# A spectral block kernel on one core: the height transform back in three runs of 128 channels instead of four of 96, and the second biases moved to a map added to x

## The reference, cut to what matters

```python
v    = group_norm(x, 32 groups)                 # mean and variance over pixels and 12 channels
bias = v @ bias_w.T + bias_b
xf   = rfftn(v.reshape(B, H, W, 4, 96), axes=(1, 2), norm='ortho')
r1 = relu(xr @ w1[0] - xi @ w1[1] + b1[0])      # per block of 96 channels
i1 = relu(xr @ w1[1] + xi @ w1[0] + b1[1])
r2 = r1 @ w2[0] - i1 @ w2[1] + b2[0]
i2 = r2 @ w2[1] + i1 @ w2[0] + b2[1]            # r2, not r1: the imaginary part uses the new real part
out = x + irfftn(complex(r2, i2), norm='ortho') + bias
```

## Time and profile before

| | us |
|---|---|
| three executions | 445.85, 444.65, 444.74 |
| median | 444.74 |
| span of the profiled execution, first to last instruction | 443.0 |
| median less that span | 1.7 |
| mean granted TensorE clock | 0.981 of full speed |
| PE busy | 411.8 (93%) |
| PE weight loads busy | 375.5 (85%) |
| DVE busy | 318.4 (72%) |
| ACT busy | 239.8 (54%) |
| POOL busy | 7.2 (2%) |
| DMA | 32.5 MB, mean 73 GB/s |

### The profile page before, as it was taken

How to read it: one execution, slowest core, us unless ns; L and a number is a source line. 1 busy time by engine, 2 the same in 40 slices (tenths; PEclk the granted TensorE clock), 3 DMA queues, 4 the chain that set the end, 5 groups by cost and what they waited for, 6 DMA issues and landing times.

```text
span 443.0 us, 17840 instructions
## 1 busy us (share of the span) xinstructions
PE 411.8 (93%) x7832; PEld 375.5 (85%) x7832; DVE 318.4 (72%) x772; ACT 239.8 (54%) x568; POOL 7.2 (2%) x13
## 2 busy tenths in 40 slices
PE   4468699989999999999999999999999999998996
PEld 4457699889998899888998899888998899987894
DVE  3679895759776876769767786768857687668734
ACT  2654785257742685438752586438752577425620
POOL 0131000000000000000000000000000000000000
PEclk9759899999999999999999999999999999999999
DMA  7570000170004300170003500161002600030004
GB/s 216 164 216 2 2 1 4 63 261 3 3 23 157 148 1 5 38 285 3 3 12 123 194 1 4 38 243 45 2 5 88 236 1 4 27 155 3 4 4 144
DMA packets 11645, 32.50 MB, mean 73 GB/s; under 512 B 4196, under 2 KB 5904, under 8 KB 11568
## 3 DMA queue, kind: packets, MB, share of 16 engines
q1 hardware_dynamic: 11568, 31.36, 20.1%
HBM read 15.63 MB, written 12.58 MB: 64 GB/s over the span
## 4 chain that ended last, share of the span: by engine, by line
PE 81%; issue 7%; DVE 6%; SPq 2%; POOL 2%; ACT 1%; DVEq 0%; POOLq 0%
PE bank L535 81%; SPq L490 1%; DVE r L1022 1%; DVE z L947 1%; DVE rsum L1015 1%; SPq L495 1%; POOL g L806 1%; ACT biasw L857 1%; DVE o_sb L1037 0%; DVE rho L947 0%; POOL g L807 0%; ACT z L863 0%; ACT yraw L823 0%; DVE extreme L1175 0%; DVE extreme L1180 0%
## 5 line engine op out<-in xcount | busy, mean ns | idle before, releaser
L535 PE MATMUL bank<-biasw,y 128*64 128x384 f16 x1152 | 108.8, 335 | 0.0
L535 PEld LDWEIGHTS bank<-biasw,y 128*64 128x64 f16 x1152 | 93.5, 196 | 1.7 <-DVE rsum L1015 0.3
L535 PEld LDWEIGHTS bank<-w2s,rho 96*64 96x64 f16 (+1 forms) x3072 | 81.4, 109 | 4.4 <-issue 2.5
L535 PE MATMUL bank<-w2s,rho 96*64 96x96 f16 (+1 forms) x3072 | 84.5, 207 | 0.0
L863 ACT ACTIVATE z<-bank 128x384 f16<-128x384 f32 x72 | 35.2, 488 | 60.5 <-PE bank L535 59.9
L535 PE MATMUL bank<-w1R,y 128*32 128x96 f16 (+3 forms) x768 | 60.1, 228 | 7.6 <-ACT y L843 3.2
L848 ACT ACTIVATE g<-bank 128x384 f16<-128x384 f32 x64 | 31.0, 484 | 64.2 <-PE bank L535 64.2
L535 PE MATMUL bank<-tab,x_sb 128*128 128x128 f32 x384 | 52.5, 291 | 11.2 <-DMA x_sb<-in_x 6.6
L535 PEld LDWEIGHTS bank<-tab,x_sb 128*128 128x128 f32 x384 | 48.3, 201 | 14.6 <-issue 7.4
L947 DVE SCALAR_TENSOR_TENSOR rho<-bank,rho 96x64 f16<-96x64 f32 (+1 forms) x128 | 50.6, 431 | 10.9 <-PE bank L535 9.2
L947 DVE SCALAR_TENSOR_TENSOR z<-bank,z 128x384 f16<-128x384 f32 x72 | 39.9, 557 | 25.6 <-ACT z L863 25.2
(11 more groups left out here) (102 smaller groups left out, 379.0 us busy)
## 6 DMA issues: line engine op xcount, KB each, us to landing
x_sb<-in_x SPq DMA_DIRECT2D x16, 768.0 KB, 7.1
out<-o_sb SPq DMA_DIRECT2D x14, 768.0 KB, 3.8
y<-y SPq DMA_DIRECT2D x24, 128.0 KB, 2.7
out<-o_sb SPq DMA_DIRECT2D x8, 192.0 KB, 1.9
tab<-in_tab SPq DMA_DIRECT2D x1, 642.0 KB, 5.9
o_sb<-in_bias_wt SPq DMA_DIRECT2D x4, 144.0 KB, 2.8
b1s<-in_b1h SPq DMA_DIRECT2D x1, 384.0 KB, 5.3
o_sb<-in_w SPq DMA_DIRECT2D x2, 144.0 KB
```

The source lines that it names most:

```text
L535: return nc.tensor.matmul(o, lhsT, rhs, start=start, stop=stop, **kw)
```

## The change

1. p4 takes `r` in three runs of 128 channels, not four of 96. There are 6 steps of 12 matmuls (72 an image) and two last steps. `rho` has 128 partitions; its tiles are three runs for each half of the units, so the middle tile holds channels of two blocks.
2. The last two steps (unit 8) become, for each half, two groups of 12 matmuls of 96 columns: first four pieces of 64 partitions (`WIDE_PIECES`), then four of 32 (`SMALL_PIECES`), 48 an image. The table `xi` is 192 wide, not 132.
3. The second weights follow: `w2s` is 128 rows in 4 slots, zero where a channel isn't of the block. `c2_rho` still has 48 matmuls of 96 columns for each gi (24 more for gi = 0), now 128 rows high. The w2 products are 16, not 8. DVE makes all forms, in 12 instructions; POOL's three are gone.
4. b2 and bias_b leave the weights and `rho`. At the start PE makes a map from them (5 matmuls, f32), DVE writes it to `added` (4 instructions), and POOL adds it to x in place, two instructions for each image, as soon as p1 of that image has read x. `add_x` waits for it. The marks' 8 loads are replaced by 3 loads, at the same place in SP's queue.
5. PE waits for those loads and for DVE's `shift_rows` before image 0. POOL's copy and memset before the second maximum, and DVE's two copies in `second_scales`, are gone. DVE's memsets at the start change tiles (zeros for the new forms, for `rhoX` and for the last 32 partitions of the two short units of `r`), and the table loaded at line 491 grows from 326 to 583 words a partition.

The core of the diff:

```diff
+WIDE_PIECES = ((0, 0, 64, 0, 0, 0), (1, 0, 64, 0, 1, 32), (1, 64, 128, 1, 0, 0), (2, 64, 128, 1, 1, 32))
+SMALL_PIECES = ((0, 64, 96, 0, 0, 64), (0, 96, 128, 0, 1, 0), (2, 0, 32, 1, 0, 64), (2, 32, 64, 1, 1, 0))
...
         def w2_loads():
+            for tile, first, last, k, ri, ch in LOAD_PIECES:
+                of = w2[ri].rearrange("(p k) c n -> k c p n", k=2)[k][ch:ch + last - first]
+                yield w2raw[first:last, :, tile, :], of
...
             load(1, 1)
-            for dst, src in mark_loads():
-                sp.dma_start(dst, src).then_inc(marks_in, 16)
+            with nc.allow_non_contiguous_dma(reason="one column of 96 per block"):
+                for dst, src in shift_loads():
+                    sp.dma_start(dst, src).then_inc(shift_in, 16)
...
             def p4(b, p, more, first):
-                for j in range(10):
-                    if j == 4:
+                for j in range(8):
+                    if j == 3:
                         c2_bias(b, p, 0 if more else 2, more, first)
...
-                    if j in (0, 4, 8):
-                        pe.wait_ge(rh_ready, 9 * b + min(j + 4, 9))
-                        pe.wait_ge(rl_ready, 9 * b + min(j + 4, 9))
+                    if j in (0, 3, 6):
+                        pe.wait_ge(rh_ready, 9 * b + (4, 8, 9)[j // 3])
+                        pe.wait_ge(rl_ready, 9 * b + (4, 8, 9)[j // 3])
...
+                            o = bank.rearrange("k (c u m) -> k c u m", u=4, m=4)[:, :, t, :]
+                            last = mm3(o, [r[:, s, u, 128 * ti:128 * ti + 128] for s in range(2)],
+                                       [heightT[:, s, int(u in SHORT_UNITS), :] for s in range(2)], True, True, skip_group_check=True)
                     else:
-                        for c in range(2):
-                            blk = 2 * (j - 8) + c
-                            last = mm3(bank[0:BC, 132 * c:132 * c + 132], [r[:, s, 8, BC * blk:BC * blk + BC] for s in range(2)],
-                                       [xi[:, s, :] for s in range(2)], True, True)
+                        half = j - 6
+                        for pieces in (WIDE_PIECES, SMALL_PIECES):
+                            for of, w in ((0, 0), (0, 1), (1, 0)):
+                                for tile, first_row, last_row, k, ri, ch in pieces:
...
             pe.wait_ge(w2_in, 16 * N_W2)
...
+            last.then_inc(w2_prod, 1)
+            pe.wait_ge(shift_in, 16 * N_SHIFT)
+            pe.wait_ge(added_ready, 1)
+            mm(c_bank[2][:, 0:CH], T("impulse", 2), b2rows[:, :], True, False, skip_group_check=True)
+            for blk in range(BLOCKS):
+                last = mm(c_bank[2][:, BC * blk:BC * blk + BC], b2row0[:, blk, :], w2imag[:, blk, :], False, blk == BLOCKS - 1, skip_group_check=True)
+            last.then_inc(shift_prod, 1)
             image(0, 0, first=True)
...
-            pool.wait_ge(w2_in, 16 * N_W2)
-            pool.wait_ge(consts_in, 16)
-            do(nc.gpsimd.tensor_copy(w2_form(0, BC, 0), by_group(w2raw[0:BC, :, 0, :])))
-            do(nc.gpsimd.tensor_scalar(w2_form(0, BC, 1), by_group(w2raw[0:BC, :, 1, :]), -1.0, None, ALU.mult))
-            do(nc.gpsimd.tensor_scalar(w2_form(BC, 3, 0), by_group(w2raw[BC:BC + 3, :, 0, :]), rowscale[BC:BC + 3, :], None, ALU.mult))
             pool.wait_ge(second_largest, 2)
-            do(nc.gpsimd.tensor_copy(extreme[BC:BC + 3, 4:5], extreme[BC:BC + 3, 2:3]))
-            do(nc.gpsimd.memset(extreme[BC:BC + 3, 2:3], 0.0))
             pool.wait_ge(s1_ready, 1)
-            do(nc.gpsimd.tensor_tensor(extreme[:, 2:5], extreme[:, 2:5], coef[:, 2:5], ALU.mult))
-            do(nc.gpsimd.tensor_scalar(extreme[:, 3:5], extreme[:, 3:5], s1[:, :], None, ALU.mult))
-            all_peak(extreme[:, 2:5], peaks2[:, :])
+            do(nc.gpsimd.tensor_tensor(extreme[:, 2:4], extreme[:, 2:4], coef[:, 2:4], ALU.mult))
+            do(nc.gpsimd.tensor_scalar(extreme[:, 3:4], extreme[:, 3:4], s1[:, :], None, ALU.mult))
+            all_peak(extreme[:, 2:4], peaks2[:, :])
+
+            pool.wait_ge(added_ready, 6)
+            for b in range(BATCHES):
+                pool.wait_ge(y_prod, Y_ITEMS * (b + 1))
+                tiles = x_sb[b % 2]
+                nc.gpsimd.tensor_tensor(tiles[:, 0, :], tiles[:, 0, :], added[:, 0, :], ALU.add).then_inc(x_shifted, 1)
+                nc.gpsimd.tensor_tensor(tiles[:, 1:TILES, :], tiles[:, 1:TILES, :], added[:, 1:2, :].to_broadcast([128, TILES - 1, CH]), ALU.add).then_inc(x_shifted, 1)
...
+            def shift_rows():
+                dve.wait_ge(shift_in, 16 * N_SHIFT)
+                row0 = T("row0", BC).rearrange("k (o m) -> k o m", o=1).to_broadcast([BC, BLOCKS, 128])
+                nc.vector.tensor_tensor(b2row0[:, :, :], row0, b2col[:, :].rearrange("k (b o) -> k b o", o=1).to_broadcast([BC, BLOCKS, 128]),
+                                        ALU.mult).then_inc(added_ready, 1)
...
             for ct in range(NT):
                 y_low(0, 0, ct)
             second_forms()
+            shift_rows()
+            shift_all()
             image(0, 0, first=True)
```

More of the change, by code:

```diff
@@ L188, in constants @@
     put("const", np.broadcast_to(const, (128, 64)))
[L189 to L206, removed]
+    sign = np.ones((128, 3))
+    for tile, first, last, _, ri, _ in LOAD_PIECES:
+        if ri:
+            sign[first:last, tile] = -1
+    put("sign", sign)
+    put("coef", np.broadcast_to([1, 2.0 ** -8, 1, 2.0 ** -7], (128, 4)))
+    whole = np.ones((SIDE, SIDE // 2 + 1))
+    real, imag = (np.fft.irfftn(c * whole, s=(SIDE, SIDE), norm="ortho")[0] for c in (1, 1j))
+    impulse = np.zeros((2, 128))
+    impulse[0, 0:SIDE] = real
+    impulse[1, 0:SIDE] = imag
+    put("impulse", impulse)
+    put("row0", np.broadcast_to(impulse[1], (BC, 128)))
+    marks = np.zeros((1, 2))
     tab = tab.astype(np.float32)
@@ L377, in spectral_block_kernel @@
         const = T("const")
-        rowscale = T("rowscale")
+        sign = T("sign")
         coef = T("coef")
@@ L409, in bias_loads @@
             yield biasraw[3:128:4, :, :], bias_wt[288:384, :].rearrange("(i b) n -> i b n", b=3)
-        def mark_loads():
-            for blk in range(BLOCKS):
-                yield rho[BC:BC + 3, 0, blk, 0, :, :].rearrange("k t m -> k (t m)"), marks_d[:, 0:640]
-                yield rhoX[BC:BC + 3, 0, blk, 0, :], marks_d[:, 640:704]
-        N_W1, N_B1, N_W2, N_BIAS, N_MARK = (len(list(loads())) for loads in (w1_loads, b1_loads, w2_loads, bias_loads, mark_loads))
+        N_W1, N_B1, N_W2, N_BIAS, N_SHIFT = (len(list(loads())) for loads in (w1_loads, b1_loads, w2_loads, bias_loads, shift_loads))
         N_ZERO = 6
@@ new lines, in shift_rows, with shift_all @@
+            def shift_rows():
[3 more added lines that the diff above has]
+                                        ALU.mult).then_inc(added_ready, 1)
+            def shift_all():
+                dve.wait_ge(shift_prod, 1)
+                for a in range(2):
+                    for of in range(2):
+                        parts = []
+                        for v in (added[:, a, :], bias_all[:, :], c_bank[2][:, 0:CH]):
+                            if len(parts) == 0:
+                                v = v.rearrange("k (c i q) -> k c i q", c=3, q=4)
+                                parts.append(v[:, :, :, 0:3] if of == 0 else v[:, :, :, 3])
+                            elif of == 0:
+                                parts.append(v[:, 0:3 * BC].rearrange("k (c i q) -> k c i q", c=3, q=3))
+                            else:
+                                parts.append(v[:, 3 * BC:CH].rearrange("k (i c) -> k c i", c=3))
+                        if a == 0:
+                            made = nc.vector.tensor_tensor(parts[0], parts[1], parts[2], ALU.add)
+                        else:
+                            made = nc.vector.tensor_copy(parts[0], parts[1])
+                        made.then_inc(added_ready, 1)
+                nc.vector.memset(newton[:, 0:1], 0.0).then_inc(added_ready, 1)
```

200 lines of the change are left out of this document (106 added, 94 removed).

## The result

The changed kernel takes 455.62 us (median of four, 454.49 to 457.21), the kernel before 444.69 beside it on the same chip (441.99 to 445.85). The ratio is 1.0255, 95% interval 1.021 to 1.0299: slower, by 10.9 us, where the forecast was slower by 4.4. The profiled execution has a span of 454.4, against 443.0.

The account below looks back on a forecast made before the run. PE bounds steady images; DVE and POOL carry the start. Span 443.0 + 11.2 (start) - 6.8 (images), additions 0, = 447.4; with 1.7 outside it, 449.1 us, slower by 1%; range 441 to 470.

Parts of the forecast that it names:

- rival A: In p4, DVE's r splits stand while POOL's long addition runs; 7 x 3.4 = +24, 473 us; chance 0.15.
- Rival D: In p4, small pieces run one after another at 0.056, so the images lose 14 against the forecast: 463 us; chance 0.05.
- images -6.8: Eight images: p4 0.72 us shorter in each (5.8), plus 1.0 from the last image's vanished wait; bounds -3.3 and -9.8.
- start +11.2: Up to scaling of bias_w: +6.0 map's chain, +6.0 POOL's routine load, -0.8 dropped copies and memset; bounds +8 and +15.
- additions 0: POOL's additions to x in each image: hidden, costing the span nothing.
- The map added by POOL: POOL's additions, 7 to 14 us an image, are hidden; DVE loses 0.1 to 0.5 an image off its path, taken 0.
- Two of the signs: Wrong if POOL's load precedes its wait, r splits or c2_rho stand behind additions, or p4 isn't shorter.
- rival B: At the start, POOL's routine load is issued ahead of the wait, or isn't needed; start +5.2, 443.1 us; chance 0.12.
- The other +6.0: At the start, POOL's routine load is issued behind its wait for second_largest and so joins the chain; between 6.00 and 8.45.
- p4: Steady image: fewer matmuls less small pieces and division changes give 0.72 us less; bounds 1.1 and 0.29.
- The last image: PE's wait of 1.02 there goes, since DVE has fewer steps; 1.0 us gained.

Follow-up runs that it names:

- e1: Changed kernel without POOL's additions of the map to x and DVE's wait for them, map still made; 441.65 us, ratio to the kernel before 0.9892.
- e8: Kernel before, with POOL adding a map of zeros to x as the change does and add_x waiting for it; 460.07 us, ratio 1.0339.
- e2: Changed kernel with POOL's additions in eight instructions of 384 elements, not one of 384 and one of 2688; 445.11 us, ratio to before 0.9991.
- e11: Changed kernel, map made later, POOL's whole additions from the second image on held until that image's low y halves are split; 440.9 us, ratio to before 0.9915.

## Where the prediction was right, and where it was wrong

The direction held, and 455.6 is in the range of 441 to 470, which was this wide for rivals A and D. The forecast itself, 449.1, was 6.5 too low: the loss is 10.9 us, two and a half times the 4.4 forecast. That it came this near, and on the right side, is luck, since its errors had opposite signs. Its terms of the span against the runs: images -6.8, measured -9.2 (some 0.9 of it PE's pauses); start +11.2, measured +5.5 (both from e1 against before); additions 0, measured +15.1 (454.4 - 439.3). So 447.4 - 2.4 - 5.7 + 15.1 = 454.4.

**The step that failed** is "The map added by POOL": "some 0.1 to 0.5 us an image on DVE, off its path in p4. Taken 0." Measured, the additions cost 9.0 in image 0, 5.6 in the six next (4.3 of waits, the rest PE's pauses) and 0.4 in the last (after less e1). Two of the signs that the prediction had named for being wrong came: `c2_rho` stands behind the additions, and POOL's configuration lies ahead of its wait. Three things in the step were wrong.
- The witness was read on one side. During the third split of y a POOL scaling ran, and I noted that DVE lost 0.24. But the scaling took 2.55, and POOL's next one, of as many elements a partition, took 1.58 with no split beside it; the same scaling in e8, where it began after the splits, took 1.55. So POOL lost 1.0. (The 0.86 that I compared with is a copy's, and makes the loss look larger.) It began at 26.21, inside the second split, as the rows of the kernel before show, two of the three splits and POOL's next scaling:

```profile
26.07 1.28 DVE L947 SCALAR_TENSOR_TENSOR y<-yraw,rstd,y 128x1024 f16<-128x1024 f32 x1
...
27.27 1.52 DVE L947 SCALAR_TENSOR_TENSOR y<-yraw,rstd,y 128x1024 f16<-128x1024 f32 x1
```

```profile
28.86 1.58 POOL L807 TENSOR_SCALAR g<-o_sb,tab 3x384 f32<-3x384 f32 x1
```

  Had it stood until that split ended at 27.35, the 1.4 left would be about its own work. So the contest was in the trace, paid mostly by the engine that came second. That the third split overlaps the rest of the scaling and loses only 0.24 doesn't fit turns by whole instructions; no run explains it. I had written "a contest that POOL loses" in rival A, and did not ask what happens when POOL comes first, with an instruction of 6 us.
- I looked for victims only among the splits of `r`. The steady victim is the copy of a third (0.24 to 4.13), and one split of `r` beside the short addition (0.56 to 1.25); in image 0 it is the split of the second weights (1.81 to 7.40) and again the copy (5.06). All read nothing but SBUF.
- I costed one steady image and multiplied. Image 0, where two images' additions follow each other at once and DVE is the engine behind, costs as much as twelve steady ones (9.0 against 0.72), with the lower clock that followed PE's wait.

**Rival A** (0.15) had the mechanism, and its size was wrong the other way: "7 x 3.4 = +24". DVE does lose some 4 us an image, but in p4 it has 1.5 of idle time and a slack that grew from 0.5 to 1.8 just as I had said, so 0.7 is left. The Trainium skill, "SBUF — State Buffer", section "SBUF: two separate sides", says that the pair of ports shared with GpSimd goes to whoever starts first, for the whole instruction, and that on DVE's side instructions with two SBUF inputs and those in a two-port performance mode are concerned. The traces agree in the cases beside a long addition: two inputs (w2s 7.40, `r` 8.54 for three, xs 5.92), a plain copy (4.13), and none with an input in PSUM. The third split of y, above, is the one row that doesn't fit. The page deserved more than 0.15.

**The start**: +6.0 from the map's chain was right (c1 at 36.21 for 35.3, forms done at 32.2 for 32.1, DVE's second maximum over at 44.6 for 44.3); the product took 3.36 rather than 2.4, at clock 0.50. The other +6.0, "the load is issued behind it. So it moves onto the chain", was wrong: the configuration goes out at 12.9, ahead of the wait. That was rival B's first half. From that maximum to the scaling 9.66 were spent for 10.41, the -0.8 of the forecast.

**p4**: forecast -0.72, measured -0.84. Unit 8's 48 matmuls with all five changes of division take 1.36 (174.37 to 175.73); forecast 0.60 + 0.32 + 0.4 + 0.1 = 1.42. Rival D (the small pieces run one after another) is refuted by this row. The Trainium skill, "TensorEngine Tiling (Array Packing)", section "Key Properties", has each change of mode drain the engine; the row agrees, as with free changes the sum would be near 0.9. An image without pauses gains more than p4, 50.53 to 49.57 = 0.96 (e1); the other 0.1 lies in the `c2_rho` stages, whose 48 matmuls, now 128 rows high, are each stage 0.01 to 0.03 shorter.

**The last image**: the wait of 1.02 for `rhoX` is gone, as forecast.

## What to carry to other kernels

Before work moves to an engine that was idle, write down which memory each of its instructions reads and which instructions of the neighbour run at that hour; here a long instruction on POOL held up VectorE's copies within SBUF and its instructions with two inputs there, by up to its whole length, and cost nothing beside a reduction or beside instructions that read PSUM. Look for the contest on both engines' rows: the one that comes second is the one that seems slow. If such work has to be moved, cut it short (14.0 us became 3.5), put it beside the neighbour's PSUM work (the steady loss became 0), and cost the first image by itself.

## What the runs showed of the hardware

- POOL is slowed too: 2688 elements take 5.88 undisturbed, 6.69 in the steady images, and an addition of 384 takes 2.51 behind a DVE instruction of 7.40.
- A change of the array's division costs, by the starts of the single records in image 2, about 0.09 from the whole to halves and about 0.1 between halves and quarters (0.136 from start to start, where neighbouring pairs follow at 0.036).
- In each of the eleven executions of the table PE pauses for 0.8 to 2.3 us at least once in c1's small unit, most often in image 4, and the trace names nothing that it waits for. In e2 and e11, where the pause was over 2 us, the granted clock then fell (mean 0.56 and 0.66 over the next 7 and 5 us), and that image took 54.5 and 52.8 where its neighbours took 49.6. So a c1 to c1 of a single image is read from an undisturbed one, and e2's six images owe some 5 of their 302.6 to this, those of the kernel before 2.2, of the changed one 2.6 and of e1 1.3. Its cause was not looked into.
